# A three-layer decoder kernel: the cross layer's key product set between two projections on TensorE, and the first projection emptied ahead of a normalisation on ScalarE

## The reference

```python
x = x + attn(layernorm(x))          # causal linear attention, 16 heads of 8
x = x + xattn(layernorm(x), ctx)    # auto-correlation attention against a context
x = x + ffn(layernorm(x))           # rms_norm, top-2 of 8 experts, gated MLP

# attn: q, k = fmap(x@wq+bq), fmap(x@wk+bk); v = x@wv+bv; fmap(y) = y+1 if y>0 else exp(y)
#   S_t = sum_{s<=t} k_s v_s^T ; z_t = sum_{s<=t} k_s ; out_t = (q_t S_t)/(q_t z_t + eps) ; out@wo+bo
# xattn: q = x@Wq+bq ; k, v = ctx@Wk+bk, ctx@Wv+bv
#   mean_value = circular correlation of q and k, averaged over heads and channels
#   index = top 4 lags of mean_value's mean over the batch; v shifted by each lag, weighted by softmax
```

## Time and profile before

| what | value |
|---|---|
| median of 3 runs | 732.22 us |
| lowest and highest of them | 729.41 and 734.09 us |
| the profiled execution | 728.99 us |
| its span, first to last instruction | 726.8 us |
| mean granted TensorE clock, share of full speed | 0.936 |
| busy share of PE, DVE, POOL, ACT over the span | 83%, 73%, 60%, 54% |
| loop of slots 4 to 13 | about 87 to 260 us of the span |

### The profile page before, as it was taken

The page is one execution under the profiler, slowest core; times in us unless marked ns, Lnnn a source line. Parts: engine busy times, 40 slices in busy tenths (PEclk is TensorE's granted clock), DMA queues, the critical chain, the costliest instruction groups (busy, mean ns, idle before and its releaser), DMA issues.

```text
span 726.8 us, 14240 instructions
## 1 busy us (share of the span) xinstructions
PE 603.2 (83%) x3196; PEld 401.4 (55%) x3197; DVE 528.1 (73%) x1794; ACT 395.6 (54%) x993; POOL 439.2 (60%) x510
## 2 busy tenths in 40 slices
PE   3889998999999998614677753699999999999995
PEld 1545555555555555313666653367666666666663
DVE  4799999988999889354588979466665666656662
ACT  3545656566656664401576552255566666656662
POOL 5999988888888884101344520555265666655652
PEclk9999999999999999655899975799999999999998
DMA  5500111000320011635545410111011111111110
GB/s 143 172 2 10 47 33 29 29 29 29 67 48 29 29 30 30 87 58 175 138 114 132 110 55 23 38 46 42 20 42 42 45 42 45 41 41 41 45 42 22
DMA packets 50609, 40.67 MB, mean 56 GB/s; under 512 B 21827, under 2 KB 40899, under 8 KB 50566
## 3 DMA queue, kind: packets, MB, share of 16 engines
q1 hardware_dynamic: 45574, 29.62, 16.0%
q0 software_dynamic: 4992, 10.56, 5.6%
HBM read 27.29 MB, written 12.88 MB: 55 GB/s over the span
## 4 chain that ended last, share of the span: by engine, by line
PE 48%; DVE 17%; issue 14%; POOL 10%; ACT 5%; DMA 3%; POOLq 1%; DVEq 0%; SPq 0%; ACTq 0%
PE bank L1081 41%; PE bank L1296 4%; ACT xh L574 2%; POOL qk L466 2%; POOL shared L471 2%; DVE R L731 2%; POOL rs_c L452 2%; PE bank L1085 1%; PE bank L1281 1%; DVE st_e L716 1%; DMA shared<-xs_d,row_u 1%; DVE best_at L895 1%; DVE mean_all L827 1%; DVE X L923 1%; DVE nd L737 1%
## 5 line engine op out<-in xcount | busy, mean ns | idle before, releaser
L1081 PE MATMUL bank<-w_s,shared 128*128 (+1 forms) x312 | 148.9, 600 | 0.3
L471 POOL TENSOR_TENSOR shared<-v,qk 128x1152 f32<-128x1152 f32 x64 | 140.9, 2201 | 12.4 <-POOL qk L466 5.5
L1081 PE MATMUL bank<-shared,tri_s 128*128 128x360 f32 (+1 forms) x384 | 135.7, 490 | 2.2 <-DVE R L731 2.2
L525 POOL DMA_INDIRECT shared<-xs_d,row_u x92 | 88.5, 962 | 67.7 <-DVE row_u L991 30.3
L1049 DVE SCALAR_TENSOR_TENSOR hid<-bank,gt,shared 128x256 f32<-128x256 f32 x156 | 75.3, 484 | 49.0 <-ACT shared L675 47.8
L731 DVE TENSOR_TENSOR R<-bank,qk 128x360 f32<-128x360 f32 (+1 forms) x192 | 96.9, 549 | 19.1 <-PE bank L1081 16.5
L532 POOL DMA_INDIRECT out_x<-shared x64 | 63.1, 985 | 72.3 <-DVE shared L1073 55.7
L675 ACT ACTIVATE shared<-bank 128x256 f32<-128x256 f32 x156 | 60.0, 385 | 78.7 <-PE bank L1081 78.6
L1081 PEld LDWEIGHTS bank<-shared,tri_s 128*128 128x128 f32 x384 | 69.9, 192 | 45.3 <-issue 25.7
L737 DVE TENSOR_REDUCE nd<-R 128x144 f32<-128x1152 f32 x64 | 86.6, 1353 | 2.6
L1081 PE MATMUL bank<-w_s,ct 128*128 (+1 forms) x624 | 82.5, 275 | 0.1
(11 more groups left out here) (213 smaller groups left out, 1088.5 us busy)
## 6 DMA issues: line engine op xcount, KB each, us to landing
xs_d<-xs SPq DMA_DIRECT2D x16, 270.0 KB, 3.5
X<-in_x SPq DMA_DIRECT2D x16, 256.0 KB, 2.8
ct<-in_ctx_t SPq DMA_DIRECT2D x16, 256.0 KB, 2.9
gram_d<-gd SPq DMA_DIRECT2D x16, 256.0 KB, 2.4
ct<-in_ctx_r SPq DMA_DIRECT2D x16, 256.0 KB, 3.6
circ<-prob_d SPq DMA_DIRECT2D x32, 64.0 KB, 2.8
w_s<-in_w_up SPq DMA_DIRECT2D x1, 2048.0 KB, 8.6
shared<-xs_d,row_u POOLq DMA_INDIRECT x92, 2.6
```

The lines of the kernel that those rows point to most:

```text
L471: nc.gpsimd.tensor_tensor(outer[k], v9[k % 2][:].unsqueeze(3).broadcast_to([P, H, D1, D]), kk.unsqueeze(2).broadcast_to([P, H, D1, D]), AL ...
L525: nc.gpsimd.indirect_dma_start(xg[q], None, xs_d[:, :], bass.IndirectOffsetOnAxis(ap=rows, axis=0)).then_inc(xg_in[q], 16)
L1081: return nc.tensor.matmul(o, l, r, start=start, stop=stop, skip_group_check=True)
```

## The change

Two moves, none of which adds or removes an instruction. On PE, in a slot that has both stage a1 and stage d (slots 2 to 14), the projection of tile 0 now comes ahead of the key product instead of behind it. On ACT the emptying of that projection now comes ahead of the normalisation `xh2` of stage d instead of behind it.

```diff
@@ scalar, slot
                 if a1:
                     a_evac_xT(*a1)
+                if a1:
+                    a_evac_proj(*a1, 0)
                 if d:
                     g, p, r = d
                     need(act, d_tr, g)
                     norm(g, p, rs_c, nb_c, c_nb, xh2, d_xh)
-                if a1:
-                    a_evac_proj(*a1, 0)
                 if c:
@@ tensor, slot
                 if b:
                     running_sums(*b, 1)
+                if a1:
+                    if i is None and a1[0] == 0:
+                        pe.wait_ge(setup, 5)
+                        pe.wait_ge(bias_ch, 8)
+                    project(*a1, 0)
                 if d:
                     g, p, r = d
                     pe.wait_ge(ct_in[p], 16 * r + 16)
                     need(pe, d_qT, g)
                     mm(bank[7][:], wk2_s[:], ct[p][:]).then_inc(d_k, 1)
                 if a1:
-                    if i is None and a1[0] == 0:
-                        pe.wait_ge(setup, 5)
-                        pe.wait_ge(bias_ch, 8)
-                    project(*a1, 0)
                     project(*a1, 1)
```

## The result

The changed kernel took 723.36 us (median of 5 runs, 719.20 to 724.69), the kernel before 730.30 us in 5 runs beside it; the ratio is 0.9876 [0.9838, 0.9914]. The profiled execution took 719.20 us with a span of 717.0 us. The forecast was 728.1 us with 723.5 as its low end, so the median lies 0.14 us under the range. The gain is 6.9 us where 4.1 us had been worked out. The forecast started from 732.22 us, the median of three runs; with two more the kernel before itself came out 1.9 us lower, and that too moved the result towards the low end.

What follows compares the result with a forecast made beforehand. POOL was taken to bound the loop at 17.28 us a slot. Entry 0.71, loop 0, exit wait 2.05 and collision 1.3 summed to 4.1 us, so 732.22 us would become 728.1, range 723.5 to 733.5.

Steps and rivals of the forecast that it cites:

- POOL as the pace of the loop: Steady loop: POOL, never stopping, sets 17.28 us a slot; PE and DVE are slaved to it.
- PE was the bound: Rival, loop: PE's waits set the pace, so removing them gives 11 us, 721 us; chance 0.10.
- The steady loop's gain of 0: Ten loop slots at POOL's own pace: no POOL instruction is touched, so 0 us gained.
- the slower rival: Loop: with DVE over 2.0 us ahead, `on` meets POOL's third outer product; 732.6 to 734.6 us, chance 0.13.
- The prediction's own sign, an iteration under 34.2 us: Profile after, loop: an iteration shorter than 34.2 us would mean POOL wasn't the bound.
- What stops DVE: Loop: `rs_c` would stop `on` first, at a DVE lead near 0.6 us, costing POOL no more than now.
- The entry: First loop slot: POOL's wait for the exponential of tile 0 goes, gaining 0.71 us.
- The exit: From slot 14 DVE is the late engine; its removed wait gains 2.05 us and a dissolved collision 1.3 us.
- The wait of 2.05 us: Slot 14: DVE's wait for PE's sums of tile 2 goes, as PE comes 2.26 us earlier.
- the collision of 1.42: Slot 15: `on`, 2.11 instead of 0.69 us, passes ahead of POOL's last outer product; 1.3 us taken.
- upper bound: Exit: if DVE too has come ahead by 1.7 us, the whole gain is 5.8 us.
- The fall of the clock: Pipeline's end: the granted clock halves at 296 us; one group earlier or later means about 2 us either way.

Runs made afterwards that it cites:

- before_on1: The kernel before with DVE forming `on` by a one-input reduction, the division left out; 743.58 us, ratio 0.9938 to the kernel before.
- pe_only: The kernel before with only the PE move, projection of tile 0 ahead of the key product; 747.97 us, ratio 0.9993.
- after_den1: The changed kernel with `den` formed by a reduction, the added constant left out; 724.04 us, ratio 0.9894 to the kernel before.
- nb_clean: The changed kernel with the sign change moved from POOL to ACT, `den` and `on` by reductions (division left out); 719.62 us, ratio 0.9826 to the kernel before.
- act_only: The kernel before with only the ACT move, tile 0 emptied ahead of the normalisation; 743.53 us, ratio 0.9937.

## Why the prediction fell short

- **POOL as the pace of the loop: right for the kernel before.** Its spacings of 0.99 and 2.14 us stood unchanged, and before_on1 shortened the loop with PE's waits left standing. The rival "PE was the bound", which would also have ended near 721 us, is refuted by that run and by pe_only.
- **The steady loop's gain of 0, since "the edit doesn't touch one POOL instruction": this step failed.** It measured 1.69 us in nine slots. The working had the row for it, the feature map of 1.12 instead of 0.73 us, but it was used as a price of the slower rival and not as a cost that a DVE lead removes. From the forecast's own numbers: `on` began 0.16 us ahead of the feature map and takes 0.69, so a lead of some 0.5 us clears it; DVE came ahead by 1.0 and 1.3 us. That POOL can't gain held only for its instructions at their free durations. The prediction's own sign, an iteration under 34.2 us, came true (34.03) and was read wrongly in it: it doesn't show that POOL wasn't the bound, since POOL's iteration without meetings is 34.1 us in the old order too (before_on1).
- **What stops DVE: wrong.** The forecast let `rs_c` stop `on`. The rows show `on` (157.13) beside `rs_c` (156.80, 1.04 us) with neither longer. `den` was stopped by the third outer product. On the exclusion the Trainium skill, "SBUF — State Buffer", SBUF: two separate sides, names VectorE instructions in a two-port mode beside those with two SBUF inputs; the stretched one-input `den` agrees with that, though no run here shows in which mode it ran; `on` beside `rs_c` doesn't agree with its rule for every GpSimd instruction that reads SBUF.
- **The entry: right**, 0.80 us for 0.71, and pe_only shows that it is the projection's earlier start that gives it.
- **The exit: right in mechanism, too small.** 4.77 us instead of 3.35 = 2.05 + 1.3. The wait of 2.05 us and the collision of 1.42 went as described, though `on` before hadn't ended just when the outer product was over, as the prediction says, but 0.54 us later (281.56 against 281.02). The missing 1.42 us is for 1.10 the lead with which DVE leaves the loop: `on` starts 0.61 us behind the last `ve_c` (259.19 against 258.58), and 1.71 us before (262.21 against 260.50). The forecast had this lead in its upper bound, as 1.7 us, and not in its sum, though it had worked out itself that DVE would gain its waits in the loop.
- **The slower rival: real, and one instruction away.** after_den1 shows it; `den`'s own stop keeps it out.
- **The fall of the clock:** its 2 us either way were too narrow. The stretch took 42.02 to 46.27 us in executions of the changed kernel.

With the two terms as they were measured, the loop's 1.69 and the lead's 1.10, the sum would have been 4.1 + 2.8 = 6.9 us, where 7.26 was measured. Left open: what sets the point at which the clock falls, and whether a complete kernel can reach nb_clean's 33.1 us an iteration, since the two places tried for the division didn't.

## What to carry to other kernels

When two engines can hold each other, the cost of a meeting stands in the duration of an instruction and not in any wait; compare each instruction with its shortest copy, and ask of every edit that shifts one engine against the other which meetings it dissolves or makes. Work taken off the pacing engine can cost time: three kernels with less work on POOL ran 0.7 to 1.1% longer than the kernel before, with the division inside an outer product; for one of them nb_clean shows that the meeting is the loss. A wait off the critical path is worth removing if it sets the phase, and a lead gained in a loop is paid out where the loop ends.

## What the runs showed of the hardware

- A one-input addition of 64 elements (`den`, 0.21 us) was held up to 1.77 us in the mean by POOL's outer products; formed by a reduction it took 0.26 us inside one too (after_den1, at 189.56 in the outer product of 189.18). `on` as a product of two inputs took 2.09 us in the mean where it met one, as a reduction 0.69 (nb_clean, at 154.79 in the outer product of 153.93).
- POOL's power instruction (1.04 us for 128x4) ran beside `on` without either growing, while the 0.20 us product behind it took 0.64 when `on` had just begun (act_only, next rows).

```profile
162.42 0.69 DVE L753 TENSOR_TENSOR on<-nd,rden 128x512 f32<-128x512 f32 x1
162.53 0.64 POOL L455 TENSOR_TENSOR mr_c<-mv_c,rs_c 128x4 f32<-128x4 f32 x1
```

- The two executions of the changed kernel did the same work, and the granted clock left 1.00 in microsecond 286 of one and 303 of the other; the stretch around it differed by 4.25 us.
